# Delta in two PSUM banks, the turned maxima in other banks, and DMA in halves with at most two in flight, in a fused attention and LoRA kernel

## The chip, the cores and the metric

The kernel runs on one core of a Trainium2 chip. The time is device microseconds of the whole kernel, weights and activations read from HBM and the result written back. It is measured three times for the kernel before; the median counts.

## What is computed

Both stages work on x of shape (8, 512, 2048). Cut to what matters:

```
x = x + xattn(layernorm(x), ctx, ctx)     # 8 heads, dh = 64 channels
    # q softmax over dh; k = ctx, softmax over the 2048 positions of its channel
    # kvs = einsum('bnhd,bnhe->bhde', k, v);  out = einsum('bnhd,bhde->bnhe', q, kvs)
x = x + ffn(layernorm(x))                 # per row: 4 experts, the best 2 of them
    # logits = flat @ router_w.T ; gates = softmax of the top 2
    # mid = einsum('tf,erf->ter', flat, A);  delta = gates * (mid @ B) * 4
```

The layernorm runs over the 2048 columns and has no weights.

## The kernel before

The 4096 rows (batch and channel) are 32 tiles of 128 partitions; a tile holds two heads of 64 channels. Each tile exists three times in HBM: x as it is (`x`), turned in chunks of 128 columns (`xt`), and the turned context (`ctxt`), with a column of ones for the sums. The turned tiles are 128 positions on the partitions by 16 chunks of 128 channels. One tile of x or xt is 1 MB, one of ctxt slightly more, and so is the output: four transfers of 1 MB per tile.

Work is cut into **quarters**: a tile has four quarters g of 4 chunks (512 columns). Every engine runs its own loop over a step number q (from -8 to 153), and in each step does the quarter that is due for each stage, a fixed number of steps apart. For tile t, stage by stage:

- q = 4t - 8: DVE takes channel maxima of ctx (`max_part`, L611); q = 4t - 4: PE turns them (`turn_max`, L355), DVE reduces them to one value per channel (`max_whole`, L620); q = 4t - 3: PE spreads that over the partitions (`spread_kmax`, L362), ACT copies it to `kmax_row` (`spread_row`, L492), and POOL subtracts it from ctx (`shift`, L304), quarter after quarter.
- q = 4t - 4: ACT sums x (`sum_x`, L499) for the layernorm, as soon as the whole tile of x has landed.
- q = 4t: ACT's exponentials (`keys`, L514; `queries`, L521) and PE's `kv` (L377) into `kv_ps`. ACT copies the result to `kv_sb`.
- q = 4t + 5: PE's `numerator` (L396) into `num_ps`, DVE's `normalise` (L671, L674) to `attnT`, and POOL adds it to the turned x in `y_sb` (`add_x`, L316).
- q = 4t + 7: PE's `project` (L413) multiplies y with router and A into `raw_ps`. ACT squares y, DVE adds halves (L652), PE sums (L426, L436).
- For two tiles together (a pair p) the gates are made on DVE, POOL and ACT in the steps after 8p + 17, and the gated middle is turned (L445) to `midT`.
- q = 8p + 21 + i, i from 0 to 7: PE's `delta` (L459, L460) multiplies two chunks of B, as high and low part, with `midT` into `delta_ps`, four matmuls of 256 columns, and DVE adds them to `y_sb` (`add_delta`, L683). `delta_ps` is one bank, so delta i + 1 waits for the addition i (L455).

Buffers: 4 tiles of ctx and of x, 8 of y, 2 of the exponentials. PSUM has 8 banks, all used: `kv_ps` 2, `raw_ps` 2, `num_ps` 2, `delta_ps` 1, `turn_ps` 1, which holds both turned maxima.

**SyncE issues every transfer**, in order. A prologue issues the first tiles at once (ctx 0 to 3, x 0 to 2, y 0 and 1, weights and constants). Then at each step q it issues a store, an x load, a ctx load and a y load of one quarter each (256 KB; `PIECES = 4`), each after a wait for the compute that releases its buffer: `delta_done` and `out_made`, `num_done`, `kv_done`, `raw_done` and `out_stored`. No load waits for another load. The last pair of tiles is stored by `store_last` (L244), 256 KB for each i.

```
for q in range(FIRST, LAST + 1):          # PE's order in a step
    delta(*delta_at(q)); turn_max(q); spread_kmax(q); sum_squares(q)
    numerator(*tile_at(q, 5)); kv(*tile_at(q, 0)); project(*tile_at(q, 7))
    fold_squares(q); turn_mid(q)
```

## Time and profile before

| | |
|---|---|
| median of 3 runs | 490.92 us (489.4 to 492.21) |
| the profiled execution's own time | 484.94 us |
| its span in the profile | 483.1 us |
| busy | PE 395.0, DVE 379.2, POOL 378.4, ACT 360.2 us |
| mean granted TensorE clock | 0.919 of 2.4 GHz |
| DMA | 136.5 MB on SyncE's queue, 83.2% of 16 engines' span |

The profile is one execution. Its times are microseconds from the span's start. A row of the waits names who stood idle, at which line, and what released it; "issue" means that nothing the profile shows released it. "DMA to landing" is the time from the issue of a transfer until its last part has arrived.

### The profile page before, as it was taken

The page shows a single profiled execution, that of the slowest core. Times are in us where ns is not written, and L with a number is a line of the kernel's source. Part 1 is how long each engine was busy: PE and PEld are TensorE (multiplying, and loading weights), DVE is VectorE, ACT ScalarE, POOL GpSimd, SP SyncE. Part 2 cuts the span into 40 slices and gives each one's busy share as a digit, 9 for nine tenths or more (in the row PEclk, how much of TensorE's full clock was granted, in tenths as well). Part 3 has the DMA queues.
Part 4 walks back from the last instruction along what each step waited for, and adds up shares of the span by engine and source line. Part 5 has one row for each costly group of instructions (what it writes and reads, how often), then busy time and mean ns, then how long its engine had stood idle before and what let it go on. Part 6 is the DMA issues. An engine that isn't in the chain of part 4 may idle for free.

```text
span 483.1 us, 22236 instructions
## 1 busy us (share of the span) xinstructions
PE 395.0 (82%) x9448; PEld 338.9 (70%) x9448; DVE 379.2 (78%) x1013; ACT 360.2 (75%) x468; POOL 378.4 (78%) x341
## 2 busy tenths in 40 slices
PE   5378877798988797988979789798899889989664
PEld 4367766687877686877768678677688677877543
DVE  2258678899998886987979889797979889778652
ACT  2469998889888885977888879797868789774200
POOL 0467999799999896987989898997979799976300
PEclk9558899899999997988999999999979999999955
DMA  8998888589998999979798989989797979554336
GB/s 279 398 388 262 254 276 273 187 270 361 277 383 254 368 297 303 305 242 372 230 370 300 358 293 303 380 270 381 265 324 236 360 288 312 181 187 153 118 137 224
DMA packets 75282, 137.95 MB, mean 286 GB/s; under 512 B 8240, under 2 KB 10416, under 8 KB 75056
## 3 DMA queue, kind: packets, MB, share of 16 engines
q1 hardware_dynamic: 75184, 136.54, 83.2%
q8 instruction: 74, 1.21, 1.0%
q14 instruction: 24, 0.20, 0.1%
HBM read 102.95 MB, written 33.55 MB: 283 GB/s over the span
## 4 chain that ended last, share of the span: by engine, by line
PE 46%; DVE 17%; issue 13%; POOL 12%; SPq 5%; DMA 4%; ACT 2%; DVEq 0%; POOLq 0%; ACTq 0%
PE num_ps L396 11%; PE kv_ps L377 10%; PE delta_ps L459 9%; PE raw_ps L413 8%; POOL y_sb L316 6%; POOL ek_sb L304 5%; PE delta_ps L460 5%; DVE y_sb L683 5%; DVE max_n L611 2%; DMA ctx_sb<-in_ctxt_dram 2%; DVE sq_b L652 2%; PE kv_ps L426 2%; DVE attnT L674 2%; SPq L231 2%; SPq L226 2%
## 5 line engine op out<-in xcount | busy, mean ns | idle before, releaser
L316 POOL TENSOR_TENSOR y_sb<-attnT,y_sb 128x512 f32<-128x512 f32 x128 | 172.8, 1351 | 41.1 <-DVE attnT L674 26.5
L304 POOL TENSOR_TENSOR ek_sb<-ctx_sb,kmax_row 128x512 f32<-128x512 f32 x128 | 172.1, 1346 | 28.5 <-ACT kmax_row L492 28.5
L683 DVE TENSOR_TENSOR y_sb<-delta_ps,y_sb 128x512 f32<-128x512 f32 x128 | 87.8, 686 | 35.3 <-PE delta_ps L460 33.9
L396 PE MATMUL num_ps<-kv_sb,x_sb 64*64 64x65 f32 x4096 | 96.8, 230 | 17.5 <-issue 10.5
L377 PE MATMUL kv_ps<-ctx_sb,ek_sb 128*64 128x65 f32 x2048 | 96.7, 237 | 12.1 <-issue 9.3
L396 PEld LDWEIGHTS num_ps<-kv_sb,x_sb 64*64 64x64 f32 x4096 | 77.7, 139 | 35.4 <-issue 25.5
L413 PE MATMUL raw_ps<-w_sb,y_sb 128*64 128x69 f32 x2048 | 90.6, 228 | 12.0 <-issue 12.0
L611 DVE TENSOR_REDUCE max_n<-ctx_sb 128x32 f32<-128x512 f32 x128 | 86.2, 677 | 15.4 <-DMA ctx_sb<-in_ctxt_dram 15.4
L459 PE MATMUL delta_ps<-midT,b_hi 128*128 128x256 f32 x256 | 84.8, 351 | 15.6 <-DVE y_sb L683 15.2
L377 PEld LDWEIGHTS kv_ps<-ctx_sb,ek_sb 128*64 128x64 f32 x2048 | 77.0, 143 | 22.9 <-issue 10.8
L674 DVE TENSOR_TENSOR attnT<-num_ps,rden 128x512 f32<-128x512 f32 x128 | 88.5, 692 | 4.4
L413 PEld LDWEIGHTS raw_ps<-w_sb,y_sb 128*64 128x64 f32 x2048 | 77.4, 140 | 14.3 <-issue 13.6
L521 ACT ACTIVATE x_sb<-x_sb,nbias,rstd 128x1024 f32<-128x1024 f32 x64 | 78.6, 1229 | 0.0
L459 PEld LDWEIGHTS delta_ps<-midT,b_hi 128*128 128x128 f32 x256 | 51.6, 202 | 33.4 <-DVE y_sb L683 19.3
L514 ACT ACTIVATE ek_sb<-ek_sb 128x1024 f32<-128x1024 f32 x64 | 67.4, 1053 | 9.5 <-POOL ek_sb L304 9.2
L460 PE MATMUL delta_ps<-midT,b_lo 128*128 128x256 f32 x256 | 70.8, 296 | 0.0
L499 ACT ACTIVATE junk<-x_sb 128x2048 bf16<-128x2048 f32 x32 | 60.9, 1903 | 7.6 <-DMA x_sb<-in_x_dram 7.6
L506 ACT ACTIVATE junk<-x_sb,negmean 128x2048 bf16<-128x2048 f32 x32 | 63.7, 1990 | 2.2 <-DVE negmean L627 2.2
L460 PEld LDWEIGHTS delta_ps<-midT,b_lo 128*128 128x128 f32 x256 | 52.7, 206 | 0.1
L652 DVE TENSOR_TENSOR sq_b<-sq_b,sq_a 128x1024 f32<-128x1024 f32 x32 | 44.6, 1395 | 9.4 <-ACT sq_b L532 9.4
L532 ACT ACTIVATE sq_b<-y_sb 128x1024 f32<-128x1024 f32 x32 | 33.7, 1054 | 7.1 <-POOL y_sb L316 7.0
L671 DVE RECIPROCAL rden<-num_ps 128x8 f32<-128x8 f32 x128 | 25.8, 201 | 16.3 <-PE num_ps L396 15.9
(57 smaller groups left out, 345.9 us busy)
## 6 DMA issues: line engine op xcount, KB each, us to landing
ctx_sb<-in_ctxt_dram SPq DMA_DIRECT2D x128, 260.0 KB, 6.0
x_sb<-in_x_dram SPq DMA_DIRECT2D x128, 256.0 KB, 6.0
y_sb<-in_xt_dram SPq DMA_DIRECT2D x128, 256.0 KB, 5.9
out_dram<-y_sb SPq DMA_DIRECT2D x128, 256.0 KB, 5.6
sq_a<-in_bt_dram SPq DMA_DIRECT2D x1, 1024.0 KB, 11.4
w_sb<-in_wt_dram SPq DMA_DIRECT2D x1, 552.0 KB, 7.4
cst<-in_consts_dram SPq DMA_DIRECT2D x1, 145.0 KB, 2.2
```

What stands on the lines that cost most here:

```text
L304: pool.tensor_tensor(ek_sb[:, t % 2, chunks(g), :].rearrange("p (a b) c -> p a b c", b=2), ctx_sb[:, t % 4, 2 * g:2 * g + 2, 1:P + 1, :].r ...
L316: pool.tensor_tensor(y, attnT[:, g, :], y, ALU.add).then_inc(x1_made, 1)
L377: mm = pe.matmul(kv_ps[t % 2][d, h:h + DH + 1], ek_sb[:, t % 2, j, d], ctx_sb[:, t % 4, j // 2, v, j % 2], start=(j == 0), stop=(j == NCH ...
L396: mm = pe.matmul(num_ps[n, h, j * (DH + 1):(j + 1) * (DH + 1)], x_sb[d, t % 4, c * P + half * DH:c * P + (half + 1) * DH], kv_sb[d, t % 2, ...
L413: mm = pe.matmul(raw_ps[p % 2][c, odd, 0:NQ], y_sb[:, t % 8, j, c], w_sb[:, j, :], start=(odd == 0 and j == 0), stop=(j == NCH - 1), skip_ ...
L459: pe.matmul(to, b_hi[:, j * P:(j + 1) * P], midT[:, p % 2, :], start=True, stop=False)
L460: mm = pe.matmul(to, b_lo[:, j * P:(j + 1) * P], midT[:, p % 2, :], start=False, stop=True)
L514: act.activation(k, k, ACT.Exp).then_inc(ek_made, 1)
L521: act.activation(half, half, ACT.Exp, bias=nbias1[:, t % 4:t % 4 + 1], scale=rstd1[:, t % 4:t % 4 + 1]).then_inc(q_made, 1)
L611: dve.tensor_reduce(max_n[:, t % 2, c], ctx_sb[:, t % 4, :, 1 + g * 32:33 + g * 32, :].rearrange("p a c b -> p c a b"), AX.XY, ALU.max).th ...
L674: dve.tensor_tensor(attnT[:, g, :].rearrange("p (k b d) -> p b k d", b=2, d=DH), heads[:, :, :, 0:DH], rden[:].unsqueeze(3).to_broadcast([ ...
L683: dve.tensor_tensor(y, delta_ps[:].rearrange("p (j t c) -> p t j c", j=2, t=2), y, ALU.add).then_inc(out_made, 1)
```

## The change

- **PSUM.** `delta_ps` becomes two banks that take turns (i % 2), so delta i waits for the addition i - 2. `turn_ps` is gone: the turned maxima go into unused columns of `num_ps`'s first bank, the spread ones into unused columns of `kv_ps[t % 2]`. What shares a bank now gets waits of its own: `turn_max` for `normalise` of the step before, `max_whole` for the numerator, the numerator of a tile's first quarter for `kmax`, `fold_squares` for `kmax_row`.
- **Order.** PE spreads the maxima after the numerator instead of before; DVE's `max_whole` comes after `add_delta`; ACT's `keys(T, 1)` comes before `spread_row`.
- **Transfers.** `PIECES` is 2: halves of about 512 KB, and SyncE's loop goes in steps of two quarters. Its order in a step is store, x, y, ctx. Each waits also for the landing of an earlier one: the store for the last y load, x for the last ctx load, y for the last store, ctx for the last x load. The prologue issues at once, as before.

```diff
@@ -116,8 +116,8 @@
         kv_ps = [bank("kv_ps0"), bank("kv_ps1")]
         raw_ps = [bank("raw_ps0", (P, 2, 256)), bank("raw_ps1", (P, 2, 256))]
         num_ps = bank("num_ps", (P, 2, 512))
-        delta_ps = bank("delta_ps")
-        turn_ps = bank("turn_ps")
+        delta_ps = [bank("delta_ps0"), bank("delta_ps1")]
+        max_ps = num_ps[:, 0, 3 * P:4 * P]
 
         ctx_landed = [sem(f"ctx_landed{i}") for i in range(4)]
         x_landed = [sem(f"x_landed{i}") for i in range(4)]
@@ -216,7 +216,7 @@
 
         @block.sync
         def _(sp):
-            PIECES = 4
+            PIECES = 2
             CP = NCH // 2 // PIECES
             XW = N // PIECES
             YC = NCH // PIECES
@@ -265,26 +265,38 @@
             whole(load_y, 1)
             whole(load_x, 2)
             whole(load_ctx, 3)
-            for q in range(0, 4 * NT + 28):
+            STEP = 4 // PIECES
+            ctx_piece = x_piece = xt_piece = out_piece = (cst_landed, 16)
+            for q in range(0, 4 * NT + 28, STEP):
+                last = q + STEP - 1
                 p, r = divmod(q - 26, 8)
                 if 0 <= p < NP - 1:
-                    after(sp, delta_done, quarters_done(q, 21))
-                    sp.wait_ge(out_made, 8 * p + 2 * (r // 2) + 2)
-                    store(2 * p + r % 2, r // 2)
-                t, r = divmod(q + 11, 4)
+                    t, k = 2 * p + r // STEP % 2, r // (2 * STEP)
+                    after(sp, raw_done, quarters_done(q - 1, 7))
+                    sp.wait_ge(out_made, 8 * p + 8 // PIECES * (k + 1))
+                    after(sp, *xt_piece)
+                    store(t, k)
+                    out_piece = (out_stored[t % 8], 32 * (t // 8) + 16 * (k + 1))
+                t, r = divmod(q + 10, 4)
                 if 3 <= t < NT:
-                    after(sp, num_done, 4 * (t - 4) + r + 1)
-                    load_x(t, r)
-                t, r = divmod(q + 16, 4)
-                if t < NT:
-                    sp.wait_ge(kv_done, 4 * (t - 4) + r + 1)
-                    load_ctx(t, r)
+                    after(sp, num_done, 4 * (t - 4) + r + STEP)
+                    after(sp, *ctx_piece)
+                    load_x(t, r // STEP)
+                    x_piece = (x_landed[t % 4], 32 * (t // 4) + 16 * (r // STEP + 1))
                 t, r = divmod(q, 4)
                 if 2 <= t < NT:
                     after(sp, raw_done, quarters_done(q, 7))
                     if t >= 8:
                         sp.wait_ge(out_stored[t % 8], 16 * PIECES * (t // 8))
-                    load_y(t, r)
+                    after(sp, *out_piece)
+                    load_y(t, r // STEP)
+                    xt_piece = (y_landed[t % 8], 32 * (t // 8) + 16 * (r // STEP + 1))
+                t, r = divmod(q + 16, 4)
+                if t < NT:
+                    sp.wait_ge(kv_done, 4 * (t - 4) + r + STEP)
+                    after(sp, *x_piece)
+                    load_ctx(t, r // STEP)
+                    ctx_piece = (ctx_landed[t % 4], 32 * (t // 4) + 16 * (r // STEP + 1))
             for i in range(8):
                 sp.wait_ge(out_made, 8 * (NP - 1) + i + 1)
                 store_last(i)
@@ -310,7 +322,7 @@
                 if t is None:
                     return
                 if g == 0:
-                    pool.wait_ge(y_landed[t % 8], 64 * (t // 8 + 1))
+                    pool.wait_ge(y_landed[t % 8], 32 * (t // 8 + 1))
                 pool.wait_ge(attn_made, 4 * t + g + 1)
                 y = y_sb[:, t % 8, chunks(g), :].rearrange("p j c -> p (j c)")
                 pool.tensor_tensor(y, attnT[:, g, :], y, ALU.add).then_inc(x1_made, 1)
@@ -351,15 +363,16 @@
                 if t is None or g:
                     return
                 pe.wait_ge(max_made, 4 * t + 4)
-                after(pe, row_made, t)
-                pe.transpose(turn_ps[:, 0:P], max_n[:, t % 2, :], ident).then_inc(maxT_done, 1)
+                after(pe, attn_made, 4 * (t - 3) + 3)
+                pe.transpose(max_ps, max_n[:, t % 2, :], ident).then_inc(maxT_done, 1)
 
             def spread_kmax(q):
                 t, g = tile_at(q, -3)
                 if t is None or g:
                     return
                 pe.wait_ge(kmax_made, t + 1)
-                pe.transpose(turn_ps[:, P:2 * P], kmax[:, t % 2:t % 2 + 1].to_broadcast([P, P]),
+                after(pe, kv_copied, t - 1)
+                pe.transpose(kv_ps[t % 2][:, P:2 * P], kmax[:, t % 2:t % 2 + 1].to_broadcast([P, P]),
                              ident).then_inc(kmaxT_done, 1)
 
             def kv(t, g):
@@ -384,6 +397,7 @@
                     return
                 if g == 0:
                     pe.wait_ge(kv_copied, t + 1)
+                    pe.wait_ge(kmax_made, min(t + 3, NT))
                 if g % 2 == 0:
                     pe.wait_ge(q_made, 2 * t + g // 2 + 1)
                 after(pe, attn_made, 4 * t + g)
@@ -420,6 +434,7 @@
                     return
                 pe.wait_ge(sq_halved, t + 1)
                 after(pe, kv_copied, min(t + 2, NT))
+                after(pe, row_made, min(t + 4, NT))
                 for k in range(2):
                     for s in range(4):
                         at = (4 * k + s) * P
@@ -452,10 +467,10 @@
                     if p == 0:
                         pe.wait_ge(b_hi_made, 1)
                         pe.wait_ge(b_lo_made, 4)
-                after(pe, out_made, 8 * p + i)
+                after(pe, out_made, 8 * p + i - 1)
                 for k in range(2):
                     j = 2 * i + k
-                    to = delta_ps[:, k * 2 * P:(k + 1) * 2 * P]
+                    to = delta_ps[i % 2][:, k * 2 * P:(k + 1) * 2 * P]
                     pe.matmul(to, b_hi[:, j * P:(j + 1) * P], midT[:, p % 2, :], start=True, stop=False)
                     mm = pe.matmul(to, b_lo[:, j * P:(j + 1) * P], midT[:, p % 2, :], start=False, stop=True)
                 mm.then_inc(delta_done, 1)
@@ -472,11 +487,11 @@
             for q in range(FIRST, LAST + 1):
                 delta(*delta_at(q))
                 turn_max(q)
-                spread_kmax(q)
                 sum_squares(q)
                 if q == 1:
                     sum_w()
                 numerator(*tile_at(q, 5))
+                spread_kmax(q)
                 kv(*tile_at(q, 0))
                 project(*tile_at(q, 7))
                 fold_squares(q)
@@ -489,12 +504,12 @@
                     return
                 act.wait_ge(kmaxT_done, t + 1)
                 after(act, shifted, 4 * (t - 1))
-                act.activation(kmax_row[:, t % 2, :], turn_ps[:, P:2 * P], ACT.Copy).then_inc(row_made, 1)
+                act.activation(kmax_row[:, t % 2, :], kv_ps[t % 2][:, P:2 * P], ACT.Copy).then_inc(row_made, 1)
 
             def sum_x(t):
                 if not 0 <= t < NT:
                     return
-                act.wait_ge(x_landed[t % 4], 64 * (t // 4 + 1))
+                act.wait_ge(x_landed[t % 4], 32 * (t // 4 + 1))
                 after(act, x_squared, t)
                 act.activation(junk[:], x_sb[:, t % 4, :], ACT.Copy,
                                accum_out=x_sum[:, t % 4:t % 4 + 1]).then_inc(x_summed, 1)
@@ -580,8 +595,8 @@
                     copy_kv(T - 1)
                     sum_x(T + 1)
                 if r == 1:
+                    keys(T, 1)
                     spread_row(T + 1)
-                    keys(T, 1)
                     square_x1(T - 2, 1)
                     queries(T - 1, 1)
                 if r == 2:
@@ -605,7 +620,7 @@
                 if t is None:
                     return
                 if g == 0:
-                    dve.wait_ge(ctx_landed[t % 4], 64 * (t // 4 + 1))
+                    dve.wait_ge(ctx_landed[t % 4], 32 * (t // 4 + 1))
                     after(dve, maxT_done, t - 1)
                 c = slice(g * 32, (g + 1) * 32)
                 dve.tensor_reduce(max_n[:, t % 2, c], ctx_sb[:, t % 4, :, 1 + g * 32:33 + g * 32, :].rearrange("p a c b -> p c a b"), AX.XY,
@@ -616,8 +631,9 @@
                 if t is None or g:
                     return
                 dve.wait_ge(maxT_done, t + 1)
+                after(dve, num_done, 4 * (t - 3) + 4)
                 after(dve, kmaxT_done, t - 1)
-                dve.tensor_reduce(kmax[:, t % 2:t % 2 + 1], turn_ps[:, 0:P], AX.X, ALU.max).then_inc(kmax_made, 1)
+                dve.tensor_reduce(kmax[:, t % 2:t % 2 + 1], max_ps, AX.X, ALU.max).then_inc(kmax_made, 1)
 
             def ln1_mean(q):
                 t, g = tile_at(q, -3)
@@ -680,7 +696,7 @@
                     return
                 dve.wait_ge(delta_done, 8 * p + i + 1)
                 y = y_sb[:, pair_slots(p), 2 * i:2 * i + 2, :]
-                dve.tensor_tensor(y, delta_ps[:].rearrange("p (j t c) -> p t j c", j=2, t=2), y,
+                dve.tensor_tensor(y, delta_ps[i % 2][:].rearrange("p (j t c) -> p t j c", j=2, t=2), y,
                                   ALU.add).then_inc(out_made, 1)
 
             def gate_centre(p):
@@ -791,14 +807,14 @@
                 if b is not None:
                     gate_beats(b, 1)
                     gate_mask(b)
-                if not early:
-                    max_whole(q)
                 mid_low(q)
                 add_delta(*delta_at(q))
                 if a is not None:
                     gate_logits(a)
                 if b is not None:
                     gate_rank(b)
+                if not early:
+                    max_whole(q)
                 normalise(*tile_at(q, 5))
                 if a is not None:
                     gate_below(a)
```

SyncE's queue in the steady part, before (8 rows are two steps of one quarter each):

```order
L239 DMA out_0_dram<-y_sb 128x512 [waits out_made,delta_done]
L231 DMA x_sb<-in_x_dram 128x512 [waits num_done]
L226 DMA ctx_sb<-in_ctxt_dram 128x520 [waits kv_done]
L235 DMA y_sb<-in_xt_dram 128x512 [waits out_stored4,raw_done]
L239 DMA out_0_dram<-y_sb 128x512 [waits out_made,delta_done]
L231 DMA x_sb<-in_x_dram 128x512 [waits num_done]
L226 DMA ctx_sb<-in_ctxt_dram 128x520 [waits kv_done]
L235 DMA y_sb<-in_xt_dram 128x512 [waits out_stored4,raw_done]
```

and with the change (8 rows are two steps of one half each):

```order
L239 DMA out_0_dram<-y_sb 128x1024 [waits y_landed0,out_made,raw_done]
L231 DMA x_sb<-in_x_dram 128x1024 [waits ctx_landed0,num_done]
L235 DMA y_sb<-in_xt_dram 128x1024 [waits out_stored3,out_stored1,raw_done]
L226 DMA ctx_sb<-in_ctxt_dram 128x1040 [waits x_landed3,kv_done]
L239 DMA out_0_dram<-y_sb 128x1024 [waits y_landed1,out_made,raw_done]
L231 DMA x_sb<-in_x_dram 128x1024 [waits ctx_landed1,num_done]
L235 DMA y_sb<-in_xt_dram 128x1024 [waits out_stored2,out_stored1,raw_done]
L226 DMA ctx_sb<-in_ctxt_dram 128x1040 [waits x_landed0,kv_done]
```

The four transfers of a step are twice as large, y has moved ahead of ctx, and every transfer waits for the landing of another kind.

PE at the first delta of a pair and the spread of the maxima, before:

```order
L459 MATMUL delta_ps<-midT,b_hi 128x256 [waits out_made,lo_made]
L460 MATMUL delta_ps<-midT,b_lo 128x256
L459 MATMUL delta_ps<-midT,b_hi 128x256
L460 MATMUL delta_ps<-midT,b_lo 128x256
L362 MATMUL turn_ps<-cst,kmax 128x128 [waits kmax_made]
L396 MATMUL num_ps<-kv_sb,x_sb 64x65 [waits attn_made,q_made,kv_copied]
L396 MATMUL num_ps<-kv_sb,x_sb 64x65 x15
L377 MATMUL kv_ps1<-ctx_sb,ek_sb 64x65 x8
L413 MATMUL raw_ps0<-w_sb,y_sb 64x69 [waits x1_made]
L413 MATMUL raw_ps0<-w_sb,y_sb 64x69 x7
L459 MATMUL delta_ps<-midT,b_hi 128x256 [waits out_made]
```

and with the change:

```order
L474 MATMUL delta_ps0<-midT,b_hi 128x256 [waits out_made,lo_made]
L475 MATMUL delta_ps0<-midT,b_lo 128x256
L474 MATMUL delta_ps0<-midT,b_hi 128x256
L475 MATMUL delta_ps0<-midT,b_lo 128x256
L410 MATMUL num_ps<-kv_sb,x_sb 64x65 [waits q_made,attn_made,kmax_made,kv_copied]
L410 MATMUL num_ps<-kv_sb,x_sb 64x65 x15
L375 MATMUL kv_ps0<-cst,kmax 128x128 [waits kv_copied,kmax_made]
L390 MATMUL kv_ps1<-ctx_sb,ek_sb 64x65 x8
L427 MATMUL raw_ps0<-w_sb,y_sb 64x69 [waits x1_made]
L427 MATMUL raw_ps0<-w_sb,y_sb 64x69 x7
L474 MATMUL delta_ps1<-midT,b_hi 128x256 [waits out_made]
```

Delta's bank alternates, and the spread maxima are written after the numerator and into `kv_ps`.

## Rows read from the trace of the kernel before

**Rows 1.** Windows: busy us (x instructions) by engine, granted clock, DMA share, GB/s.
```profile
107.80:415.10 307.30, 266.69 (x6744) 229.75 (x6738) 265.37 (x719) 256.16 (x334) 270.80 (x241) 0.97 0.91 311
...
60.00:100.00 40.00, 30.36 (x852) 26.19 (x851) 32.09 (x86) 34.31 (x44) 36.83 (x33) 0.96 0.77 244
```

**Rows 2.** The page: granted clock, GB/s in 40 slices, queue of fetches.
```profile
PEclk9558899899999997988999999999979999999955
...
GB/s 279 398 388 262 254 276 273 187 270 361 277 383 254 368 297 303 305 242 372 230 370 300 358 293 303 380 270 381 265 324 236 360 288 312 181 187 153 118 137 224
...
q8 instruction: 74, 1.21, 1.0%
```

**Rows 3.** Waits, whole span: who for whom, us, times, longest.
```profile
PE delta_ps L459 <- DVE y_sb L683: 15.2, 25, 0.9
POOL y_sb L316 <- DMA y_sb<-in_xt_dram: 14.2, 9, 3.0
...
PE raw_ps L413 <- issue: 12.0, 11, 2.1
...
PE num_ps L396 <- issue: 10.5, 9, 3.2
...
PE kv_ps L377 <- issue: 9.3, 8, 2.0
```

**Rows 4.** DMA issues: count, KB each, median us to landing.
```profile
ctx_sb<-in_ctxt_dram SPq DMA_DIRECT2D x128, 260.0 KB, 6.0
...
cst<-in_consts_dram SPq DMA_DIRECT2D x1, 145.0 KB, 2.2
```

**Rows 5.** Waits of SyncE's queue, whole span.
```profile
SPq L286 <- DMA out_dram<-y_sb: 43.4, 12, 6.5
```

**Rows 6.** Timeline of PE around 186 us: start, us, instruction, idle before.
```profile
184.08 0.57 PE L396 MATMUL num_ps<-kv_sb,x_sb 64*64 64x65 f32 x22
187.84 0.69 PE L396 MATMUL num_ps<-kv_sb,x_sb 64*64 64x65 f32 x10 [3.19 <-issue]
```

**Rows 7.** Line 226, the one issue from 1.0 to 1.5 us.
```profile
DMA to landing us min/median/max: 2.7/2.7/2.7
```

**Rows 8.** Timeline of SyncE from 93 to 97 us.
```profile
93.69 0.33 SPq L226 DMA_DIRECT2D ctx_sb<-in_ctxt_dram  x1
94.61 0.33 SPq L235 DMA_DIRECT2D y_sb<-in_xt_dram  x1
```

**Rows 9.** Line 231, the issues from 92 to 97 us.
```profile
DMA to landing us min/median/max: 3.5/3.6/3.7
```

**Rows 10.** Line 226, the issue at 93.7 us.
```profile
DMA to landing us min/median/max: 3.1/3.1/3.1
```

**Rows 11.** Line 239, the store issued at 444.7 us.
```profile
DMA to landing us min/median/max: 2.2/2.2/2.2
```

**Rows 12.** Line 226, the five issues from 20 to 26 us.
```profile
L226 SPq DMA_DIRECT2D ctx_sb<-in_ctxt_dram x5: 510/522/1315, 21.4 to 25.1; - x5
...
DMA to landing us min/median/max: 8.8/9.0/11.3
```

**Rows 13.** Timeline of ACT, the sum of x of tile 29.
```profile
389.45 1.90 ACT L499 ACTIVATE junk<-x_sb 128x2048 bf16<-128x2048 f32 x1
```

**Rows 14.** Waits of PE from 389 to 483 us.
```profile
PE delta_ps L459 <- DVE y_sb L683: 11.7, 17, 0.9
PE raw_ps L413 <- issue: 2.5, 3, 1.6
```

**Rows 15.** Timeline of DVE, the last of the eight last additions.
```profile
479.79 0.69 DVE L683 TENSOR_TENSOR y_sb<-delta_ps,y_sb 128x512 f32<-128x512 f32 x1 [1.31 <-PE delta_ps L460]
```

**Rows 16.** Timeline of PE, two matmuls of one of these delta groups.
```profile
471.10 0.41 PE L459 MATMUL delta_ps<-midT,b_hi 128*128 128x256 f32 x1
471.31 0.41 PE L460 MATMUL delta_ps<-midT,b_lo 128*128 128x256 f32 x1
```

**Rows 17.** Waits of POOL from 107 to 416 us.
```profile
POOL ek_sb L304 <- ACT kmax_row L492: 4.0, 5, 1.9
```

## The prediction

> **What bounds the kernel now.** I read the steady stretch first, then the waits, then the transfers, then the end. From 107.8 to 415.1 us (the first kv matmuls of tiles 7 and 30) the kernel works through 23 tiles, 13.36 us each, or 6.68 us per half tile; in that stretch PE is busy 266.7 us, POOL 270.8, DVE 265.4 and ACT 256.2 of 307.3, and the DMA engines 91% at 311 GB/s [rows 1]. So no engine is full: four of them have 11.1 to 11.8 us of work per tile, and about 1.6 us per tile is lost to waiting for each other. The transfers are close behind, yet they are hardly waited for: POOL waited 14.2 us for y_sb in all [rows 3]. That is because SyncE issues far ahead. A quarter lands 6.0 us after its issue (median of the ctx loads) [rows 4]; 512 of them, four kinds of 128 each, in some 470 us make 512 x 6.0 / 470 = 6.5 transfers, 1.7 MB, in the air at a time. SyncE has waited 43.4 us for a store to land before it could load y over it [rows 5].
>
> The second thing to see is PE standing still in the middle of a group of equal matmuls, released by nothing: 12.0, 10.5 and 9.3 us, together 31.8 [rows 3]. The longest is 3.19 us between two of the 32 numerator matmuls at 187.84 us [rows 6]. Nothing in the program separates them. Queue 8 fetched instructions 74 times in the run [rows 2], and I take these gaps for fetches that came late behind the data transfers; the rows show the gap and the fetches, not the link. The Trainium skill ("Runtime: NRT & Kernel Launch", Instruction fetch mechanics) calls the cost of crossing an instruction block mostly hidden. By that rule the gaps would have another cause and the change would not touch them; the forecast below doesn't rest on them.
>
> **The change, part by part.**
>
> *Halves, two in flight.* In each round of two quarters SyncE now issues a store, an x load, a y load and a ctx load, in that order, each about 512 KB. The store waits until the last y load has landed, the y load until the store has, the x load until the last ctx load has, the ctx load until the x load has. So there are two chains, and one of them is made of loads only: x, ctx, x, ctx, each issued when the one before has landed. One round of it carries half a tile, so it needs c = landing time of x + of ctx + SyncE's turn-round. SyncE is in order; a chain that is late holds back the other three issues too. To keep today's pace c must not be over 6.68 us.
>
> What does a half take to land? No row shows one. From below: the very first ctx quarter, with only the 145 KB of constants ahead of it, took 2.7 us [rows 7], and 256 KB more take 0.66 us at 398 GB/s, the best slice [rows 2]: 3.4 us each, c = 6.9 with 0.1 for the turn-round (an estimate: a DMA instruction takes 0.33 us [rows 8], but that time lies inside the landing time). From above: around 94 us, when SyncE issued about one quarter per microsecond [rows 8] and about three were in the air (0.8 MB, less than the 1.0 MB that the change allows), x took 3.6 us [rows 9] and ctx 3.1 [rows 10]; plus 0.66 each this makes 4.3 and 3.8, c = 8.2. The store quarter at 444.7 us took 2.2 us [rows 11], so a half store takes 2.9, and the chain of store and y is the shorter one: it doesn't set the end. I take c = 7.4, a little under the middle: the transfers at 94 us had more requests beside them than two halves make, but the traffic was as mixed. Both ends stay for the range.
>
> The sum for the end of this chain: the last ctx quarters of the prologue were issued until 25.1 us and landed 9.0 us later [rows 12], so the prologue is in at about 34, and ctx half 0 of tile 4, queued behind it, at 35. Then come x, ctx, x: x of tile 3 is complete at 35 + 1.5c = 46, and x of tile t at 46 + 2c(t - 3). Up to tile 29 the ctx loads of tiles up to 31 lie between the x loads; after that the chain is free. x of tile 29 is complete at 46 + 52c = 431 us. Before, ACT began to sum it at 389.4 [rows 13]; what follows took 483.1 - 389.4 = 93.7 us. The buffers give no further slack: four ctx and four x tiles as before, released at the same quarter or one later, and an x tile is used four quarters after its last load is released.
>
> *The end of the kernel.* Delta in two banks lets PE go on while DVE adds. In the steady part the wait it removes is small: PE waited 15.2 us for DVE's add in all [rows 3], 11.7 of it after 389 us [rows 14], and the rest hides under POOL. At the end it counts: the last eight additions come every 2.0 us, 0.69 us of work after 1.31 of waiting [rows 15], because PE's four matmuls (0.21 us apart from the second on [rows 16], the clock granted there being 0.5 [rows 2], which is 1.2 GHz) and DVE's addition take turns. With two banks the pace is PE's 4 x 0.21 = 0.85 to 0.9: 8 x 1.1 = 9 us less. The last store then lands as before, some 2.5 us after the last addition. Another 2.5 us comes from the delta waits of the tile pair before that (half of 11.7 - 8 x 0.78 = 5.5), and 2.5 from the instruction gaps after 389 us [rows 14]. Together 14 us less.
>
> *The turned maxima in other banks.* PE turns the second maximum after the numerator (0.69 us later), DVE reduces after the delta addition (0.69 later), and ACT makes kmax_row after an Exp (1.05 later, of which it idled part). POOL's subtraction waits for that row; from 107 to 416 us it waited 4.0 us in five places [rows 17]. I cost this at nothing, because the loads set the pace and leave every engine over 2 us idle per tile. If that cover is gone, some 0.7 us per tile goes the other way, 20 us over 29 tiles.
>
> *Clock.* With longer tiles PE is busy 11.6 of 14.8 us, 78%. From 60 to 100 us it was busy 76% and was granted 0.96 [rows 1], so I add nothing.
>
> Sum: 431 + 93.7 - 14 = 510.5 us of span, 27.4 more than 483.1. The profiled execution's own time was 484.94, 1.8 over its span: 512.3. The median of the runs shown, 490.92, lies 6.0 above the profiled one; against it the forecast is 490.9 + 27.4 = **518 us**.
>
> **The rivals.** In each, span = 46 + 52c + 79.7, and 7.8 is added for the median.
> *Faster: a half lands as quickly as the quietest load shows.* The constants, 145 KB, landed in 2.2 us [rows 4]; 375 KB more at 398 GB/s make 3.14 us, c = 6.4: 458.5 of span, 466. The engines could follow, since without the 31.8 us of gaps a tile takes 13.36 - 1.0 = 12.4. For it: transfers with less traffic around them are quicker. Against: it leaves no collision of the two chains, which carry 311 GB/s now, and at 94 us a quarter of x, half as large, took 3.5 us at least [rows 9]. The decision falls at c = 6.87; below that the change gains. The Trainium skill ("DMA: Bandwidth & Descriptors", Anatomy of one DMA) gives 2.0 us + bytes / 436 GB/s for a transfer of another issuing path; by it a half takes 3.2 us, c = 6.5 and the time 471.5, beside this rival. No run here shows a half yet.
> *No change:* c is at its lower end, 6.9, and loss and gain cancel: 484.5 of span, 492. Or the loads are quick and the later kmax_row takes it back: 466 + 20 = 486.
> *Much slower: the chains collide.* c at or over 8.2, since every load queues behind half a store or y load and a fetch: 552 of span, 560. For it: the loads at 94 us took over 3 us with about three quarters in the air [rows 9, 10]. Against: two evenly spaced halves need the engines only 4 x 1.33 = 5.3 us of a round.
>
> **How the numbers follow.** Forecast (c 7.0 to 8.0) 0.54, much slower 0.15, faster 0.23, no change 0.08. A measurement of this kernel tells about 0.5% from no change, 2.5 us. Of the no-change case 0.05 lies within that, the rest is slower: faster 0.23, same 0.05, slower 0.72. The range 464 to 554 leaves out about half of the two outer cases; the forecast's own range is 497 to 549.
>
> **What would show it.** Right: about 256 issues of 512 KB landing in 3.4 to 4.2 us; SyncE waiting above all for DMA (x and ctx) instead of PE; ACT's sum of x and DVE's first maxima waiting for DMA; DMA share near 80%; 14 to 15 us per tile; PE's gaps without a releaser mostly gone; the last eight additions 0.9 us apart. Wrong: halves landing under 3.3 us with tiles at 12.5 us, and PE or POOL busy over 90%.

## The result: 22% slower

| | before | after |
|---|---|---|
| median | 490.16 us (487.2 to 492.21, 4 runs) | 600.98 us (593.0 to 605.0, 4 runs) |
| ratio | | 1.224 (95% interval 1.214 to 1.235) |
| span in the profile | 483.1 us | 591.2 us |
| mean granted TensorE clock | 0.919 | 0.829 |

Medians are of all runs of a kernel; ratios and their intervals compare its fast runs with the fast runs of the kernel before, measured beside them.

The direction was forecast, the size was not: 518 us, with 554 as the upper end. The sections of the page on busy time, clock, DMA queues and the chain that ended last:

```profile
PE 443.2 (75%) x9448; PEld 386.9 (65%) x9448; DVE 382.8 (65%) x1013; ACT 359.4 (61%) x468; POOL 371.6 (63%) x341
...
PEclk9568678877788978878887887887779688889988
...
GB/s 318 412 178 155 181 208 196 196 231 243 217 245 254 240 255 252 254 230 254 246 241 217 258 221 270 247 229 232 244 273 236 253 244 223 227 178 161 148 231 232
...
q1 hardware_dynamic: 38896, 136.52, 68.1%
q8 instruction: 75, 1.23, 0.9%
...
DMA 72%; PE 16%; DVE 3%; issue 2%; POOL 2%; ACT 2%; SPq 1%; DVEq 0%; ACTq 0%
```

The data queue's share of the DMA engines fell from 83.2% to 68.1%, the rate, which had swung between 230 and 383 GB/s in the middle slices [rows 2], stays between 217 and 273, and the chain that ended last is 72% DMA. The steady stretch is now 103.8 to 485.6 us, from the first raw_ps matmuls of tile 4 to those of tile 26; its row in the view by windows answers to the first of [rows 1]:

```profile
103.80:485.60 381.80, 294.37 (x6446) 258.29 (x6446) 257.70 (x693) 244.09 (x319) 254.78 (x232) 0.83 0.73 241
```

That is 22 tiles in 381.8 us: 17.35 us per tile where there were 13.36, or 8.7 us per half tile. Every engine has the work it had (PE more, at a lower clock) and waits for the rest. The issues, by line, with the KB of each and the median us to landing; the ctx row answers to [rows 4]:

```profile
ctx_sb<-in_ctxt_dram SPq DMA_DIRECT2D x64, 520.0 KB, 4.3
x_sb<-in_x_dram SPq DMA_DIRECT2D x64, 512.0 KB, 4.0
y_sb<-in_xt_dram SPq DMA_DIRECT2D x64, 512.0 KB, 4.7
out_dram<-y_sb SPq DMA_DIRECT2D x60, 512.0 KB, 3.6
```

A half is twice a quarter and lands sooner, 4.0 to 4.7 us instead of 6.0, since at most one other is in the air with it. Two halves in some 4.2 us are 1.05 MB / 4.2 = 250 GB/s: that is the rate of the slices above, and it is less than the 311 GB/s the kernel used before. The waits, who for whom, us, times, longest:

```profile
POOL y_sb L328 <- DMA y_sb<-in_xt_dram: 144.2, 30, 8.1
...
DVE max_n L626 <- DMA ctx_sb<-in_ctxt_dram: 86.1, 32, 6.8
PE raw_ps L427 <- POOL y_sb L328: 86.0, 29, 5.2
...
POOL ek_sb L316 <- ACT kmax_row L507: 46.1, 28, 11.2
ACT junk L514 <- DMA x_sb<-in_x_dram: 30.2, 24, 6.6
```

POOL's wait for y went from 14.2 us [rows 3] to 144.2. Gone are PE's gaps released by nothing: together they were 33.9 us, now 0.2. What SyncE itself waited for (line 42 is the helper that all these waits go through):

```profile
SPq L42 <- DMA x_sb<-in_x_dram: 137.3, 55, 3.9
SPq L42 <- DMA ctx_sb<-in_ctxt_dram: 127.0, 54, 4.4
SPq L42 <- DMA y_sb<-in_xt_dram: 96.0, 50, 4.4
SPq L42 <- DMA out_dram<-y_sb: 65.9, 51, 3.1
```

All four kinds of transfer are waited for, 426 us in all, in a queue that is 591 us long. And the chain of waits, around 300 us (start, us, what):

```profile
300.98 4.95 DMA out_dram<-y_sb
...
306.00 5.33 DMA y_sb<-in_xt_dram
...
311.41 3.21 DMA out_dram<-y_sb
...
314.69 4.35 DMA y_sb<-in_xt_dram
```

Store and y load follow each other without a break. Their rows are landing times: the next issue follows within 0.1 us of each landing.

### The profile page after: what moved, and what is told of

Same layout as the page of the kernel before. It is cut to its first block, busy times and chain, and to the rows that moved or that the text cites. A ratio compares the mean times of both kernels' runs of the same rounds, so it can differ in the third digit from the quotient of the medians.

```text
span 591.2 us, 22059 instructions
## 1 busy us (share of the span) xinstructions
PE 443.2 (75%) x9448; PEld 386.9 (65%) x9448; DVE 382.8 (65%) x1013; ACT 359.4 (61%) x468; POOL 371.6 (63%) x341
## 3 DMA queue, kind: packets, MB, share of 16 engines
q1 hardware_dynamic: 38896, 136.52, 68.1%
## 4 chain that ended last, share of the span: by engine, by line
DMA 72%; PE 16%; DVE 3%; issue 2%; POOL 2%; ACT 2%; SPq 1%; DVEq 0%; ACTq 0%
DMA y_sb<-in_xt_dram 32%; DMA out_dram<-y_sb 22%; DMA ctx_sb<-in_ctxt_dram 11%; DMA x_sb<-in_x_dram 7%; PE raw_ps L427 3%; PE kv_ps L390 3%; PE num_ps L410 3%; PE delta_ps L474 3%; POOL y_sb L328 2%; PE delta_ps L475 2%; PE raw_ps L481 1%; DVE y_sb L699 1%; DVE sq_b L668 1%; DVE attnT L690 1%; ACT junk L514 1%
## 5 line engine op out<-in xcount | busy, mean ns | idle before, releaser
L328 POOL TENSOR_TENSOR y_sb<-attnT,y_sb 128x512 f32<-128x512 f32 x128 | 164.7, 1288 | 147.6 <-DMA y_sb<-in_xt_dram 144.2
L427 PE MATMUL raw_ps<-w_sb,y_sb 128*64 128x69 f32 x2048 | 102.9, 252 | 86.0 <-POOL y_sb L328 86.0
L427 PEld LDWEIGHTS raw_ps<-w_sb,y_sb 128*64 128x64 f32 x2048 | 89.6, 161 | 90.3 <-issue 85.7
L410 PE MATMUL num_ps<-kv_sb,x_sb 64*64 64x65 f32 x4096 | 104.8, 249 | 17.4 <-DVE attnT L690 14.5
L390 PE MATMUL kv_ps<-ctx_sb,ek_sb 128*64 128x65 f32 x2048 | 104.7, 253 | 7.1 <-ACT ek_sb L529 7.0
L410 PEld LDWEIGHTS num_ps<-kv_sb,x_sb 64*64 64x64 f32 x4096 | 86.1, 157 | 33.0 <-issue 18.9
L390 PEld LDWEIGHTS kv_ps<-ctx_sb,ek_sb 128*64 128x64 f32 x2048 | 85.1, 158 | 20.4 <-ACT ek_sb L529 8.1
L474 PE MATMUL delta_ps<-midT,b_hi 128*128 128x256 f32 x256 | 91.2, 373 | 1.5 <-DVE midT L790 1.0
L475 PEld LDWEIGHTS delta_ps<-midT,b_lo 128*128 128x128 f32 x256 | 57.8, 226 | 0.0
L441 PE MATMUL kv_ps<-sq_b,cst 128*32 128x128 f32 x512 | 21.8, 290 | 17.9 <-DVE sq_b L668 17.9
```

What stands on the lines that cost most here:

```text
L328: pool.tensor_tensor(y, attnT[:, g, :], y, ALU.add).then_inc(x1_made, 1)
L390: mm = pe.matmul(kv_ps[t % 2][d, h:h + DH + 1], ek_sb[:, t % 2, j, d], ctx_sb[:, t % 4, j // 2, v, j % 2], start=(j == 0), stop=(j == NCH ...
L410: mm = pe.matmul(num_ps[n, h, j * (DH + 1):(j + 1) * (DH + 1)], x_sb[d, t % 4, c * P + half * DH:c * P + (half + 1) * DH], kv_sb[d, t % 2, ...
L427: mm = pe.matmul(raw_ps[p % 2][c, odd, 0:NQ], y_sb[:, t % 8, j, c], w_sb[:, j, :], start=(odd == 0 and j == 0), stop=(j == NCH - 1), skip_ ...
L474: pe.matmul(to, b_hi[:, j * P:(j + 1) * P], midT[:, p % 2, :], start=True, stop=False)
L475: mm = pe.matmul(to, b_lo[:, j * P:(j + 1) * P], midT[:, p % 2, :], start=False, stop=True)
```

## The experiments

Twelve kernels. Each is the changed kernel or the one before with the edit shown; the last five keep the changed kernel's PSUM part and have quarters. Medians of the kernel before, measured beside them, were 486.9 to 489.1 us.

### Which part of the change: PSUM and order alone

SyncE's whole loop of before in the changed kernel:

```diff
-            PIECES = 2
+            PIECES = 4
...
-                    after(sp, *xt_piece)
-                    store(t, k)
+                    store(2 * p + r % 2, r // 2)
```

> The changed kernel with the PSUM banks and the order of the change, but SyncE's loop of before: quarters, no wait of one transfer for another. Theory 1 (all of the loss is the limit on transfers in flight): no loss is left, only the faster end of the kernel, 475 to 482 us, the last eight additions about 0.8 us apart, and PE's gaps released by nothing near 30 us as before. Theory 2 (the later kmax_row and the new waits on shared banks cost some tenths of a us per tile): 492 to 515 us, with POOL waiting over 15 us for kmax_row.

Measured: 481.9 us (478.5 to 486.9), ratio 0.984 (0.977 to 0.991). Theory 1. POOL waited 35.3 us for kmax_row, which theory 2 had as its sign, but 28.5 of that is in the kernel before too. PE's gaps without a releaser were 38.9 us. The additions at the end, in DVE's timeline:

```profile
467.96 1.29 DVE L687 TENSOR_TENSOR y_sb<-delta_ps,y_sb 128x512 f32<-128x512 f32 x2 [0.46 <-PE delta_ps L463]
...
471.01 1.30 DVE L687 TENSOR_TENSOR y_sb<-delta_ps,y_sb 128x512 f32<-128x512 f32 x2 [0.23 <-PE delta_ps L463]
```

These are the first and the last of the three pairs that end it: two pairs take 471.01 - 467.96 = 3.05 us, so an addition comes every 0.76 us, where one came every 2.0 [rows 15].

### Which part of the change: the transfers alone

SyncE's loop of the change in the kernel before, with 32 for 64 in the three waits of the consumers, nothing else:

```diff
-            PIECES = 4
+            PIECES = 2
...
+                    after(sp, *ctx_piece)
+                    load_x(t, r // STEP)
...
-                act.wait_ge(x_landed[t % 4], 64 * (t // 4 + 1))
+                act.wait_ge(x_landed[t % 4], 32 * (t // 4 + 1))
```

> The kernel before with SyncE's loop of the change: halves, at most two in flight; PSUM and order as before. Theory 1: the whole loss is here, 600 to 615 us, 16.5 to 17.5 us per tile, halves landing in 4.0 to 4.7 us. Theory 2 (the two parts make it together): under 560 us.

Measured: 622.0 us (617.4 to 624.7), ratio 1.272 (1.263 to 1.281), 7 us above the upper end of what theory 1 gave. Halves landed in 4.3 (x), 4.5 (ctx), 4.8 (y) and 3.7 us (stores). So the transfers are the whole loss, and the PSUM part gives back 21 us of it, more than the 7 it gives alone. Which of its pieces gives more beside the limit was not tried.

### Halves or the limit

```diff
-                    after(sp, *xt_piece)
                     store(t, k)
...
-                    after(sp, *ctx_piece)
                     load_x(t, r // STEP)
...
-                    after(sp, *out_piece)
                     load_y(t, r // STEP)
...
-                    after(sp, *x_piece)
                     load_ctx(t, r // STEP)
```

> The changed kernel without the four waits of one transfer for another; halves stay. Theory 1 (what costs is how many bytes may be in the air): 472 to 490 us, 2 MB and more in the air, halves landing in 5 to 8 us, PE's gaps released by nothing back at 25 us or more. Theory 3 (halves themselves are the loss: later release, coarser landing, longer rows): over 540 us.

Measured: 485.6 us (477.7 to 491.2), ratio 0.982 (0.973 to 0.991). The halves cost nothing; the four waits make 115 us. PE's gaps are back at 38.7 us. Without them the transfers take longer to land and carry more:

```profile
ctx_sb<-in_ctxt_dram SPq DMA_DIRECT2D x64, 520.0 KB, 5.7
...
y_sb<-in_xt_dram SPq DMA_DIRECT2D x64, 512.0 KB, 6.5
```

### Four halves in flight instead of two

```diff
-                    after(sp, *xt_piece)
+                    after(sp, *out_piece)
                     store(t, k)
...
-                    after(sp, *ctx_piece)
+                    after(sp, *x_piece)
                     load_x(t, r // STEP)
...
-                    after(sp, *out_piece)
+                    after(sp, *xt_piece)
                     load_y(t, r // STEP)
...
-                    after(sp, *x_piece)
+                    after(sp, *ctx_piece)
                     load_ctx(t, r // STEP)
```

> The changed kernel with each half waiting for the last half of its own kind, so that four may be in flight instead of two. Theory 1: 2.1 MB at a landing time of about 6 us is 350 GB/s, enough for 12 us per tile; compute bounds again, 470 to 488 us. Rival (each wait for a landing costs by itself, since SyncE stands in order behind it): 520 us or more, SyncE waiting for DMA over 150 us.

Measured: 487.3 us (480.3 to 493.8, 10 runs), ratio 0.990 (0.985 to 0.994). The same four waits, each for the other semaphore, cost nothing that shows. SyncE waited 199.5 us for landings in its profiled run, more than the 150 that the rival gave as its sign, and the time did not move. It is not SyncE's waiting as such, it is how much it may have out.

### A half alone

```diff
-                    after(sp, *xt_piece)
+                    after(sp, *issued[-1])
                     store(t, k)
-                    out_piece = (out_stored[t % 8], 32 * (t // 8) + 16 * (k + 1))
+                    issued.append((out_stored[t % 8], 32 * (t // 8) + 16 * (k + 1)))
```

and the same for the three loads.

> The changed kernel with one transfer in flight: each half waits for the landing of the one issued just before it, of whatever kind. This measures how long a half takes alone. Theory 1a (two halves in flight hardly disturb each other; a half of a load takes over 4 us by itself): loads land in 4.0 to 4.5 us, 950 to 1050 us in all. Theory 1b (about 1 us of the 4.0 to 4.7 us is the other half's data and the rest is what the forecast took): loads land in 3.3 to 3.6 us, stores in 2.7 to 2.9, 800 to 860 us in all.

Measured: 892.8 us (one run). Its issues, median us to landing:

```profile
ctx_sb<-in_ctxt_dram SPq DMA_DIRECT2D x64, 520.0 KB, 3.6
x_sb<-in_x_dram SPq DMA_DIRECT2D x64, 512.0 KB, 3.8
y_sb<-in_xt_dram SPq DMA_DIRECT2D x64, 512.0 KB, 3.8
out_dram<-y_sb SPq DMA_DIRECT2D x60, 512.0 KB, 2.7
```

Both theories missed in time; it lies between them. The landings are nearer to theory 1b: the store's 2.7 us is in its range, the loads are at its upper end or 0.2 us over it. A half of x takes 3.8 us alone and one of ctx 3.6. Their sum is 7.4, the very c of the forecast: I had taken the value of an empty machine for that of two halves at a time. In the changed kernel they take 4.0 and 4.3, y 4.7 instead of 3.8, stores 3.6 instead of 2.7. That is 0.2 to 0.9 us each for the one other half.

### Which chain sets the pace

xc_free:

```diff
-                    after(sp, *ctx_piece)
+                    after(sp, *x_piece)
                     load_x(t, r // STEP)
...
-                    after(sp, *x_piece)
+                    after(sp, *ctx_piece)
                     load_ctx(t, r // STEP)
```

sy_free:

```diff
-                    after(sp, *xt_piece)
+                    after(sp, *out_piece)
                     store(t, k)
...
-                    after(sp, *out_piece)
+                    after(sp, *xt_piece)
                     load_y(t, r // STEP)
```

> The changed kernel with the chain of x and ctx cut (x waits for the last x, ctx for the last ctx), store and y still in one chain: three halves in flight. If the chain of loads alone set the end, as the forecast had it, this is 480 to 500 us. If the chain of store and y sets it as much, it stays at 560 us or more.

> The changed kernel with the chain of store and y cut (each waits for the last of its own kind), x and ctx still in one chain: three halves in flight. If the chain of loads alone set the end, it stays at 590 us or more. If both do, it is near xc_free, 560 us or more; if neither does alone, both come down to 500 to 540.

Measured: xc_free 556.0 us (ratio 1.140, 1.131 to 1.150), sy_free 604.8 (1.238, 1.229 to 1.247). SyncE's waits in xc_free:

```profile
SPq L42 <- DMA y_sb<-in_xt_dram: 197.3, 52, 5.3
SPq L42 <- DMA out_dram<-y_sb: 134.9, 51, 4.3
SPq L42 <- DMA ctx_sb<-in_ctxt_dram: 26.1, 11, 6.1
SPq L42 <- DMA x_sb<-in_x_dram: 16.0, 10, 2.7
```

and in sy_free:

```profile
SPq L42 <- DMA x_sb<-in_x_dram: 196.2, 55, 5.0
SPq L42 <- DMA ctx_sb<-in_ctxt_dram: 192.2, 54, 4.9
SPq L42 <- DMA out_dram<-y_sb: 22.4, 12, 3.2
SPq L42 <- DMA y_sb<-in_xt_dram: 19.2, 7, 5.0
```

xc_free is 4 us short of the 560 that stood for "the other chain as much", and far from the 480 to 500 of the loads alone; sy_free stayed over 590. Each chain alone is enough to hold the kernel 69 to 118 us above before, even with three halves in the air. Cutting the store and y chain gives nothing, cutting the loads' chain gives 45 us. Left alone, the loads' chain is the slower one by 49 us, 1.7 us per tile.

### Bytes or requests

Quarters in the order of before, each waiting for the last one of its kind (PSUM part as changed):

```diff
+                    after(sp, *x_piece)
                     load_x(t, r)
+                    x_piece = (x_landed[t % 4], 64 * (t // 4) + 16 * (r + 1))
```

> The PSUM and order part of the change with quarters of 256 KB, each waiting for the last quarter of its own kind: four in flight, the same 1 MB as two halves. If bytes in the air count, a quarter among four lands in 3.6 to 4.0 us, 15 to 16 us per tile: 540 to 580 us. If the number of requests counts, this is as fast as psum_only, 475 to 490.

Measured: 624.6 us (618.7 to 626.4), ratio 1.278 (1.268 to 1.288). The sign of "bytes" and more of it than I gave:

```profile
ctx_sb<-in_ctxt_dram SPq DMA_DIRECT2D x128, 260.0 KB, 4.3
x_sb<-in_x_dram SPq DMA_DIRECT2D x128, 256.0 KB, 4.3
y_sb<-in_xt_dram SPq DMA_DIRECT2D x128, 256.0 KB, 4.0
out_dram<-y_sb SPq DMA_DIRECT2D x128, 256.0 KB, 3.9
```

Each kind is issued once per quarter step and must land in between, so a tile takes at least 4 x 4.3 = 17.2 us. One megabyte in the air is too little however it is cut, and for quarters a little more so. The number of requests is not what counts: own4 has the same four in flight, twice as large, and loses nothing.

### A sliding window

Every quarter has its own semaphore, so that SyncE can wait for the transfer K issues back (here K = 6, against qsems, which has the semaphores but no window):

```diff
+            issued = [(cst_landed, 16)] * 6
             for q in range(0, 4 * NT + 28):
...
+                    after(sp, *issued[-6])
                     load_x(t, r)
+                    issued.append((x_landed[t % 4][r], 16 * (t // 4 + 1)))
```

qsems against psum_only: the semaphores alone, without a window, and with a y load that waits for the store of its own quarter:

```diff
-                        sp.wait_ge(out_stored[t % 8], 16 * PIECES * (t // 8))
+                        sp.wait_ge(out_stored[t % 8][r], 16 * (t // 8))
```

> psum_only with a semaphore of its own for every quarter of every buffer, so that a y load waits for the store of its own quarter and not of the whole tile. SyncE waited 37.8 us for stores in psum_only. If those waits delay loads that are needed, 470 to 478 us; if the loads are early enough without it, within 1% of psum_only, 477 to 487.

Measured: 479.8 us (477.6 to 482.6), ratio 0.984 (0.978 to 0.991), as psum_only. The waits for stores had cost nothing.

> qsems with a window: before each issue SyncE waits for the transfer eight issues earlier, so at most eight quarters (2.05 MB) are in the air. Theory 1 (rate = bytes in the air / landing time): eight land in about 6.4 us, 327 GB/s, 12.6 us per tile, no loss: 470 to 485 us. Theory of the gaps (PE's instruction fetches are late in proportion to the queue): with at most 2 MB ahead, instead of up to 3, the gaps released by nothing fall from some 38 us to under 25 and the time to 465 to 475.

Measured: 481.5 us (473.0 to 487.2), without an interval for its ratio; it can't be told from qsems. PE's gaps were 38.1 us, not under 25. That half of the expectation was wrong.

> The same with a window of six quarters (1.54 MB). Theory 1: they land in about 5.2 us, 296 GB/s, 13.9 us per tile: 495 to 515 us, and the gaps released by nothing under 12 us. Rival (a sliding window loses nothing against no limit, only the chains of four kinds did): 470 to 485 us.

Measured: 495.3 us (494.0 to 501.5), ratio 1.015 (1.009 to 1.021). Theory 1 at its lower end. The gaps were 19.9 us, more than I gave, but half of those without a window; POOL's waits for y grew meanwhile (1.7 us in qsems, 8.3 in psum_only):

```profile
POOL y_sb L328 <- DMA y_sb<-in_xt_dram: 41.8, 16, 4.4
```

### The later kmax_row

Against psum_only:

```diff
                 turn_max(q)
+                spread_kmax(q)
                 sum_squares(q)
...
                 numerator(*tile_at(q, 5))
-                spread_kmax(q)
...
-                    keys(T, 1)
                     spread_row(T + 1)
+                    keys(T, 1)
```

> psum_only with kmax_row early again: PE spreads the maxima before the numerator and ACT makes the row before its Exp; DVE's order stays that of the change. If the later row costs (POOL waited 35.3 us for it in psum_only, 28.5 in the kernel before), 2 to 6 us less than psum_only, 476 to 480; if POOL's wait only moved there from elsewhere, the same as psum_only within 1%.

Measured: 482.3 us (479.5 to 488.9), ratio 0.987 (0.979 to 0.995), the same as psum_only. POOL's wait for the row in psum_only, then here:

```profile
POOL ek_sb L304 <- ACT kmax_row L495: 35.3, 19, 12.3
```

```profile
POOL ek_sb L304 <- ACT kmax_row L495: 28.1, 8, 12.0
```

The later row does cost POOL 7 us of waiting, as feared. Without it POOL waits that much longer for attnT (26.5 us instead of 22.1) and for y (12.0 instead of 8.3), and the time doesn't move.

## Why the prediction was wrong in size

**Right: what replaces what.** The two chains, SyncE's turn-round under 0.1 us, the DMA bound in the steady part, the end of PE's gaps, and the shorter end all came. The last additions, in DVE's timeline of the changed kernel:

```profile
578.58 0.43 DVE L790 TENSOR_TENSOR midT<-raw_ps,midT 64x256 fp32r<-64x256 f32 x1 [0.35 <-ACT midT L584]
579.04 1.50 DVE L699 TENSOR_TENSOR y_sb<-delta_ps,y_sb 128x512 f32<-128x512 f32 x2
580.94 0.69 DVE L699 TENSOR_TENSOR y_sb<-delta_ps,y_sb 128x512 f32<-128x512 f32 x1 [0.40 <-PE delta_ps L475]
581.85 0.69 DVE L699 TENSOR_TENSOR y_sb<-delta_ps,y_sb 128x512 f32<-128x512 f32 x1 [0.22 <-PE delta_ps L475]
582.94 3.75 DVE L699 TENSOR_TENSOR y_sb<-delta_ps,y_sb 128x512 f32<-128x512 f32 x5 [0.40 <-PE delta_ps L475]
```

These are nine. PE starts the first delta of the last pair after the `midT` at 578.58:

```profile
579.06 0.39 PE L474 MATMUL delta_ps<-midT,b_hi 128*128 128x256 f32 x1 [0.47 <-DVE midT L790]
```

So the addition at 579.04 is the last of the pair before, and the last eight run from about 579.8 to 586.69: 6.9 us, 0.86 each, where the forecast had 0.85 to 0.9 and the kernel before 2.0 (14.7 us for its eight). That is about 8 of the 9 us of the term. The 14 us taken off the end also held 2.5 for PE's gaps, though the forecast was said not to rest on them.

**Wrong: "I take c = 7.4".** This term of the sum was mis-sized: c measured 8.6 to 8.7. It was between two ends, 6.9 and 8.2, and the truth, 8.6 to 8.7, is beyond the upper one. The number came to be the sum of two halves alone (cap1: 3.6 + 3.8). The term that was missing is the other half in the air: every x and ctx half shares the engines with a store or a y load, always, since both chains are in permanent need. The medians, 4.0 for x and 4.3 for ctx, add up to 8.3; the means of the 23 halves of each from 113 to 300 us are 4.1 and 4.4, and with two turn-rounds of under 0.1 us that is the 8.6 to 8.7 of the steady stretch. I had a hint and used it the wrong way: the loads at 94 us [rows 9, 10] were the only rows with about 1 MB in the air, and instead of taking them as the nearest row I argued a little under the middle. Their 8.2 would have given 552 + 7.8 = 560 us. The start of the chain was right: ACT found x of tile 3 landed at 45.0 us, where the forecast had 46. ACT's sums of x of tiles 3 and 29:

```profile
45.00 1.91 ACT L514 ACTIVATE junk<-x_sb 128x2048 bf16<-128x2048 f32 x1 [0.79 <-DMA x_sb<-in_x_dram]
...
492.38 1.91 ACT L514 ACTIVATE junk<-x_sb 128x2048 bf16<-128x2048 f32 x1 [2.13 <-DMA x_sb<-in_x_dram]
```

For tile 29 the forecast said 431, and (492.4 - 46) / 52 = 8.6. This step alone is 61 of the 81 us of span that were missing.

**Wrong: "the chain of store and y is the shorter one: it doesn't set the end".** Counted alone it is shorter (2.7 + 3.8 = 6.5), but in company it is 3.6 + 4.7 = 8.3, as long as x and ctx with 4.0 + 4.3. It is the one that the chain of waits runs through, and xc_free shows it holds the kernel at 556 us by itself. It shares the pace and doesn't set it alone: with it cut, in sy_free, the loads' chain still holds the kernel at 604.8. After ACT's sum the changed kernel took 591.2 - 492.4 = 98.8 us where the forecast had 79.7, and there POOL waited 20.7 us for y, against 0.3 in that part of the kernel before: y loads and stores run on in their chain. That fits the 19 us that were missing there; no run tests it by itself.

**Wrong, at a cost that no run shows: "I add nothing" for the clock.** The stretch from 60 to 100 us, 76% busy at 0.96, was the nearest row and misled. In the steady stretch after, PE is 77% busy and is granted 0.83. One of PE's pauses in its timeline, and the granted clock after it in the view by windows (the last column but two):

```profile
312.81 1.19 PE L427 MATMUL raw_ps<-w_sb,y_sb 128*64 128x69 f32 x16 [5.20 <-POOL y_sb L328]
...
318.60 0.69 PE L410 MATMUL num_ps<-kv_sb,x_sb 64*64 64x65 f32 x32
```

```profile
312.80:317.00 4.20, 4.19 (x63) 3.93 (x65) 1.67 (x6) 3.06 (x4) 4.20 (x4) 0.50 0.85 232
318.50:322.00 3.50, 3.50 (x105) 2.94 (x105) 2.92 (x14) 3.50 (x6) 3.35 (x3) 1.00 0.87 296
```

After 5.2 us of idling it goes on at 0.5, which is 1.2 GHz (16 matmuls of raw_ps in 1.19 us), and from 318.5 us it has the full 2.4 GHz again (the 32 of the numerator in 0.69). Whether this costs time was not tested by itself. That the DMA bound hides most of it is likely and not shown; dma_only, with longer pauses, has a similar clock, 0.821.

**The rivals.** "Much slower: the chains collide", chance 0.15, is what happened; its 560 is still 40 short, and the fetch that it also named is not shown. The faster rival fell with cap1: even alone a half of x or ctx takes 3.6 us or more (medians), so two of them do not reach c = 6.4. The Trainium skill's 2.0 us + bytes / 436 GB/s ("DMA: Bandwidth & Descriptors", Anatomy of one DMA) gives 3.2 us for a half, for another issuing path than SyncE's. The traces here differ: 3.6 to 3.8 for a load alone and 2.7 for a store (cap1), so for these loads it is about 0.5 us too quick, and with another half in the air (3.6 to 4.7) it is further off.

## What to carry to other kernels

A limit on transfers in flight is a limit on the rate: bytes in the air divided by the landing time that they have in each other's company, not alone. Compare it with the rate the kernel uses now. Here 1.05 MB at 4.2 us make 250 GB/s against 311 needed, while 1.5 MB cost 1.5% and 2 MB nothing. Where transfers wait for each other in a chain, sum the landing times link by link for each chain, and take them from the trace at the traffic that the change will have.

## What the runs showed that I had not expected

PE's gaps released by nothing shrink where fewer data transfers are in the air. They were 34 to 43 us in the kernels with up to 2 MB or more (before, psum_only, psum_rowfirst, uncapped, own4, qsems, qcap8), 19.9 at six quarters, 10.4 and 5.0 at three halves, 1.0 and 0.2 at two, and none in cap1 and quarters_own. That they are instruction fetches stays an inference: the number of fetches hardly changed (74 and 75). That the transfers make them is not shown either. PE's other waits go the opposite way in the same kernels: 36 to 50 us where the gaps are 34 to 43, 68 at six quarters, 113 and 154 at three halves, 142 in the changed kernel. A PE that stands still for something else may hide a late fetch as well. And in the kernel before there is no such gap until 60 us, though the prologue's loads are in the air then: PE has done 732 matmuls by that time and stood 19.9 us for other things. No run separates the two. In any case the gain in the gaps never paid: a limit low enough to close them starves the kernel first. The Trainium skill ("Runtime: NRT & Kernel Launch", Instruction fetch mechanics) calls the cost of going on to the next block of instructions mostly hidden. If the gaps are fetches, 34 to 43 of 476 to 492 us were not hidden here in the kernels with up to 2 MB or more in the air.

The version that beats both is the PSUM part without the limit: 0.984 with quarters (psum_only, qsems), 0.982 with halves (uncapped), each with an interval that ends at 0.991.
